# Re-planned stages in a wavelet convolution block with vector quantization: branch order, interleaved attention products, two upper-band steps on GpSimd, loop written out

## The reference

```python
x = x + conv_block(_gn(x), ...)      # _gn: per image and channel, mean and variance over all pixels
x = x + vq(_gn(x), codebook)

def conv_block(x, ...):
    LL, LH, HL, HH = _dwt_haar(x)                      # four 64x64 bands of 32 channels
    hf = concat([LH, HL, HH])
    x1 = lrelu(conv(lrelu(conv(hf, w15)), w25))        # 5x5
    x2 = lrelu(conv(lrelu(conv(hf, w13)), w23))        # 3x3
    x3 = lrelu(conv(lrelu(conv(hf, w12)), w22))        # 2x2
    y = lrelu(conv(x1 + x2 + x3, wd1, dil=2))          # then wd2, wd3, also dilated
    alpha = sigmoid(conv(y, wca))                      # 1x1, to 3 * 32 channels
    phf = alpha * hf
    z = batchnorm(conv(concat([LL, phf]), wcb))        # 3x3
    return _idwt_haar(z * sigmoid(z), conv(phf, whf), HL, HH)

def vq(x, codebook):                                   # 512 codes of 32 channels
    idx = argmin(|x|^2 - 2 x.codebook^T + |codebook|^2)
    return codebook[idx]
```

## Time and profile before

| | us |
|---|---|
| time, three runs | 2281.72, 2288.87 (median), 2294.78 |
| span of the profiled execution | 2164.4 |
| median less span | 124.5 |
| mean granted clock of TensorE | 0.951 |

### The profile page before, as it was taken

One profiled execution on the slowest core, in us unless ns is written; L12 is line 12 of the kernel. 1 busy time (PEld: TensorE's weight loads), 2 busy tenths in 40 slices (PEclk: granted clock), 3 DMA queues, 4 the chain that ended last, 5 costly groups with the idle time before them and its releaser, 6 DMA issues. The chain is left out here.

```text
span 2164.4 us, 27115 instructions
## 1 busy us (share of the span) xinstructions
PE 1984.8 (92%) x5232; PEld 946.5 (44%) x5232; DVE 1810.3 (84%) x3979; ACT 1059.2 (49%) x2018; POOL 1252.3 (58%) x1299
## 2 busy tenths in 40 slices
PE   6999999999999999999999999999999999995653
PEld 3444455444544455444544445444544445442221
DVE  4122799988999799988999899988999889888996
ACT  5134645545555545546556454546455454543331
POOL 2001277654776377663776367673776457673876
PEclk9999999999999999999999999999999999995555
DMA  6000011111110112111111111111111011110111
GB/s 203 15 10 5 20 40 43 27 29 34 46 35 21 41 36 47 25 24 41 42 36 26 42 35 41 30 24 37 43 41 26 20 25 34 30 25 20 34 37 32
DMA packets 80459, 76.97 MB, mean 36 GB/s; under 512 B 29200, under 2 KB 62608, under 8 KB 80016
## 3 DMA queue, kind: packets, MB, share of 16 engines
q1 hardware_dynamic: 45776, 50.78, 8.3%
q0 software_dynamic: 32768, 16.84, 5.2%
q10 hardware_dynamic: 1728, 7.41, 0.9%
HBM read 41.36 MB, written 16.78 MB: 27 GB/s over the span
## 5 line engine op out<-in xcount | busy, mean ns | idle before, releaser
L1053 POOL DMA_INDIRECT vqc<-in_codebook,idx x1024 | 1000.9, 977 | 545.2 <-DVE idx L964 306.4
L542 PE MATMUL ring<-hf,w_sb 128*128 128x512 f32 x1824 | 888.5, 600 | 2.9 <-ACT hf L715 2.9
L487 PE MATMUL score<-cst,yst 98*128 98x512 f32 x1024 | 788.4, 777 | 83.8 <-DVE idx L964 54.8
L960 DVE MAX8 top<-score 128x8 f32<-128x512 f32 x1024 | 695.3, 684 | 74.7 <-PE score L487 63.8
L964 DVE FIND_INDEX8 idx<-top,score 128x8 uint32<-128x512 f32 x1024 | 704.2, 690 | 0.0
L666 ACT CAST yst<-bands 32x256 fp32r<-32x256 f32 x1024 | 411.3, 402 | 174.6 <-PE score L487 162.1
L542 PEld LDWEIGHTS ring<-hf,w_sb 128*128 128x128 f32 x1824 | 341.6, 191 | 316.9 <-issue 294.2
L487 PEld LDWEIGHTS score<-cst,yst 98*128 98x128 f32 x1024 | 204.0, 202 | 395.0 <-DVE idx L964 206.3
L542 PE MATMUL ring<-ha,w_sb 128*128 128x512 f32 x704 | 347.5, 598 | 5.1 <-DVE ha L853 4.6
L542 PE MATMUL ring<-hb,w_sb 128*128 128x512 f32 x544 | 262.6, 595 | 6.8 <-DVE hb L866 6.8
L627 ACT ACTIVATE z<-ring,prm 128x512 f32<-128x512 f32 x144 | 99.0, 688 | 273.3 <-PE ring L542 272.7
(11 more groups left out here) (101 smaller groups left out, 1276.8 us busy)
## 6 DMA issues: line engine op xcount, KB each, us to landing
xnat<-in_x SPq DMA_DIRECT2D x128, 128.0 KB, 2.7
yst<-yl SPq DMA_DIRECT2D x512, 32.0 KB
vqc<-in_codebook,idx POOLq DMA_INDIRECT x1024
out<-vqc SPq DMA_DIRECT2D x128, 128.0 KB
w_sb<-in_weights ACTq DMA_DIRECT2D x1, 1920.0 KB, 8.2
w_sb<-in_weights ACTq DMA_DIRECT2D x3, 384.0 KB, 12.8
w_sb<-in_weights ACTq DMA_DIRECT2D x1, 1152.0 KB, 15.6
w_sb<-in_weights ACTq DMA_DIRECT2D x1, 960.0 KB, 8.6
```

Source lines behind the costliest of these rows:

```text
L487: nc.tensor.matmul(score[BANK["tile", t]][:, :], yst[0:KST, j % 2, g, wp], cst[0:KST, :], start=True, stop=True).then_inc(s_tile, 1)
L542: t = nc.tensor.matmul(ring[g % RING][:, :, :], w_sb[:, SLOTS[n, m, kind, ky], :], own(source(n, m, kind), half, slice(PAD + di, PAD + di ...
L960: nc.vector.max(top8[:, t % 4, :], score[BANK["tile", t]][:, :]).then_inc(s_top, 1)
L1053: nc.gpsimd.indirect_dma_start(vqc[:, c % 2, w * CH:(w + 1) * CH], None, codebook[:, :], bass.IndirectOffsetOnAxis(idx[:, c % 2, k, 0:1], ...
```

## The change

The parts, in the order of the plan:

- `ORDER` becomes w13, w12, w23, w22, w15, w25, wd1, wd2, wd3. `w22` is now added to `w23` (`branch_pair`), and `w25` to both (`branch_sum`). `LEAKY_TILE` puts w13 and w15 in `ha`, w12 in `hb`.
- `mean2`, `var2`, `bias2` stand before products 8, 12, 16. DVE's steps of `finish` and `finish_rest` are spread over `finish`, `mean2` and `var2`, the last of them between `veps` and the wait for `rstd`. ACT's `high` and POOL's `low` start with `var2`.
- `normal_side` (8 ACT instructions) moves to the end of the round before, `normal_edge` (6) from there to a new step `edge` before product 40.
- A new step `upper` before product 48: POOL computes the sum and the difference of HL and HH (before: DVE, at the end of the round). DVE's statistics of them move to a new step `spread` before product 58; only the LH step stays at the last `cbmap` (`upper_low`).
- `wcb`, `wca` and `whf` are interleaved; `wca` and `whf` share the two banks of `wd3`, `wcb` has those of `wd2` (`group_banks`, `freed_before`). `weighted_sides` is cut into three steps `wside`.
- Turns: `xchunk` before tiles with t % 16 = 9, `mean1` before tile 126, `var1` behind tile 127. Turns start before product 20; the EDGE products of half 1 without turns are those of w25, wd1, wd2, wd3.
- POOL issues each gather one tile later than before, with the same rule as `index`.
- `wait_apart` becomes `wait`: no semaphore step between the wait and its instruction.
- The loop of `rounds` is written out: nine bodies with constant numbers.

```diff
-XTURN = 10
-LEAD, REAR = 9, 16
+XTURN = 9
+LEAD, REAR = 8, 16
+EDGING = 40
...
-ORDER = ["w15", "w13", "w25", "w12", "w23", "w22", "wd1", "wd2", "wd3"]
+ORDER = ["w13", "w12", "w23", "w22", "w15", "w25", "wd1", "wd2", "wd3"]
...
+def group_banks():
+
+    banks = {key: g % RING for key, g in GROUP.items() if key[0] in ORDER}
+    for h in range(2):
+        last = banks["wd3", h]
+        for m in range(3):
+            banks["wca", m, h] = last
+        banks["whf", h] = last
+        banks["wcb", h] = banks["wd2", h]
...
-            if t == TILES - 4:
+            if t == TILES - 2:
                 turns.append(("mean1",))
-            if t == TILES - 2:
-                turns.append(("var1",))
             turns.append(("tile", t))
+    turns.append(("var1",))
...
+    def attention(m):
+        return [("mm", "wca", half, m, OWN, 0) for half in range(2)]
+
+    def map_of(m, halves=(0, 1)):
+        return [("mm", "wcb", half, m, OWN, ky) for half in halves for ky in range(3)]
+
+    def high_bands(m):
+        return [("mm", "whf", half, m, OWN, 0) for half in range(2)]
+
+    plan += map_of(0, (0,)) + attention(0) + map_of(0, (1,)) + [("cbmap", 0)] + attention(1)
+    plan += map_of(1) + attention(2) + [("wside", 0), ("wside", 1)]
+    plan += map_of(2) + high_bands(0) + [("cbmap", 1)] + high_bands(1) + [("cbmap", 2), ("wside", 2)]
+    plan += high_bands(2) + map_of(3) + [("cbmap", 3)]
...
-    at = {LEAD: [("mean2",)], LEAD + 6: [("var2",)], LEAD + 9: [("bias2",)], LEAD + 10: [("side",)]}
+    at = {LEAD: [("mean2",)], LEAD + 4: [("var2",)], LEAD + 8: [("bias2",)],
+          EDGING: [("edge",)], EDGING + 8: [("upper",)], EDGING + 18: [("spread",)]}
...
-def wait_apart(eng, sem, value, passed):
-
-
-    wait(eng, sem, value)
-    eng.sem_inc(passed, 1)
...
-            with eng.Fori(0, (IMAGES - 2) // 2) as i:
-                body(2 * i + 1, 1, True, True, True)
-                body(2 * i + 2, 0, True, True, True)
+            for b in range(1, IMAGES - 1):
+                body(b, b % 2, True, True, True)
...
+            def mean2(v, par):
+                statistics(1, v, s_dq, QSTEP * v + 1, 0, vpart[:, :])
+                quarter(raw(par, LH), resid, par).then_inc(s_dh, 1)
+                dve.wait_ge(s_dh, 2 * (v + 1))
+                quarter_rest(raw(par, HL), nresid, par)
+
+            def var2(v, par):
+                dve.wait_ge(s_var[1], v + 1)
+                nc.vector.tensor_scalar_add(veps[1][:, :], score[1][:, 0:1], GN_EPS).then_inc(s_veps[1], 1)
+                quarter_rest(raw(par, HH), resid, par).then_inc(s_band, 1)
+                dve.wait_ge(s_rstd[1], v + 1)
...
+            def upper(b, par):
+
+                pool.wait_ge(s_side, b + 1)
+                pool.wait_ge(s_hfw, 6 * (b + 1))
+                wait(pool, s_band, b)
+                nc.gpsimd.tensor_tensor(hsum[:, :, :], raw(par, HL), raw(par, HH), ALU.add).then_inc(s_up, 1)
+                pool.wait_ge(s_up, b + 1)
+                nc.gpsimd.tensor_tensor(raw(par, HH), raw(par, HL), raw(par, HH), ALU.subtract).then_inc(s_upper, 1)
...
+                        if pending is not None:
+                            gather(v, pending)
+                        pending = t
+                        if t in RUN_ENDS:
+                            gather(v, t)
+                            pending = None
```

More of the change, by code:

```diff
@@ L107, with freed_before @@
 RING = 4
-assert NG % RING == 0
+def group_banks():
[6 more added lines that the diff above has]
+        banks["wcb", h] = banks["wd2", h]
+    assert len({banks["wd3", 0], banks["wd3", 1], banks["wcb", 0], banks["wcb", 1]}) == RING
+    return banks
+GBANK = group_banks()
+def freed_before(b, key):
+    g = GROUP[key]
+    held = [NG * c + h for c in (b - 1, b) for k, h in GROUP.items()
+            if GBANK[k] == GBANK[key] and 0 <= NG * c + h < NG * b + g]
+    return max(held) + 1 if held else 0
 COL = {n: i for i, n in enumerate(["b15", "b13", "b12", "b25", "b23", "b22", "bd1", "bd2", "bd3", "bca0", "bca1",
@@ L181 @@
 LEAKY = ORDER
-HAS_EDGE = ["w15", "w13", "w12", "wd1", "wd2"]
+HAS_EDGE = ["w13", "w12", "w15", "wd1", "wd2"]
 def last_products():
@@ L498, in source @@
                     return hf[m][kind]
-                return {"w25": ha, "w23": hb, "w22": ha, "wd1": hb, "wd2": ha, "wd3": hb, "wca": ha}[n][kind]
+                return {"w25": ha, "w23": ha, "w22": hb, "wd1": hb, "wd2": ha, "wd3": hb, "wca": ha}[n][kind]
             def inputs_ready(b, n, half, m, kind):
-                if n == "w15" and half == 0:
-                    pe.wait_ge(s_hfw, 6 * b + (m + 1 if kind == 0 else m + 4))
+                if n == "w13" and kind == OWN and half == 0:
+                    pe.wait_ge(s_hfw, 6 * b + m + 1)
+                elif n == "w15" and kind == EDGE and half == 0:
+                    pe.wait_ge(s_hfw, 6 * b + m + 4)
                 elif n == "w13" and kind == LEFT and half == 0:
@@ L633, in evacuate @@
                         fill.then_inc(s_edge, 1)
-                    if half == 1 and n == "w22":
+                    if half == 1 and n == "w25":
                         act.wait_ge(s_sum, 2 * b + 2)
@@ L740, in body @@
                             xorder(b + 1, k)
[L741 removed]
+                    if quant and what == "var2":
                         for j in range(2):
@@ L759, in body @@
                         normal_ll(b + 1, 1 - par)
-                    elif conv and what == "side":
-                        normal_side(b, par)
-                    elif conv and what == "cbmap" and step[1] == 1:
-                        weighted_sides(b)
+                    elif conv and what == "edge":
+                        for m in range(3):
+                            normal_edge(b, par, m)
+                    elif conv and what == "wside":
+                        weighted_side(b, step[1])
                     elif conv and what == "mm":
```

145 lines of the change are left out of this document (63 added, 82 removed).

## The result

| | before | after |
|---|---|---|
| time, median of 6 runs, us | 2288.52 (2281.72 to 2294.78) | 2264.41 (2262.23 to 2268.85) |
| ratio | 1 | 0.9886, 95% interval 0.9864 to 0.9908 |
| span of the profiled execution, us | 2164.4 | 2263.3 |
| its own time less its span, us | not known | 1.8 |

The change makes the kernel 24 us (1.1%) faster, a small gain but clear of the noise, where 22 were forecast. But its span is 99 us *longer* than the one the prediction rests on. The two can't both be taken at face value, and most of what follows is about that.

What follows compares the result with a forecast made beforehand. PE bounds the kernel, DVE a close second. Six looped rounds -20 us, round 7 -1, round 0 -0.5, round 8 -0.5: -22 in all, span 2164.4 to 2142, plus 124.5 outside: 2267 us, range 2239 to 2302.

Steps and rivals of the forecast that it cites:

- The base: Whole kernel: span 2164.4 us, median 124.5 above it and held there; 12.5 us per looped round above PE's floor to win.
- Loop written out: Rounds 1 to 6: straight code costs nothing seen; gain only the 1.86 us idle at back edges, already counted.
- Semaphore steps: Separate steps behind waits: given no price; in round 8 the 0.30 us between gathers was taken as unchanged.
- Branch order: Convolution branches: wait before `wd1` goes, 1.2 us, and score-bank waits, 2.0 us, per looped round.
- Pile-up: Tiles 3 to 31: extra DVE work stops PE about 7.3 us per looped round (5.3 to 13.5).
- GpSimd's sum and difference: Products 49 to 56: POOL's 4.3 to 5.2 us hidden; DVE held 1 us, bounds 0 and 5.2.
- rival B: Products 49 to 56: POOL's sum and difference hold DVE; slower, 2298 to 2304 us; chance 0.15.
- Start of the round: First tiles: side copies moved and mean one product earlier gain some 3.1 us per looped round.
- Attention: Attention stage: covered waits gain 1.9 us per looped round, next image's later mean 1.9, half of `attend`'s hold on DVE 1.4.
- Round 8: Last round, set by POOL's gathers: gather spacing unchanged, round stays at 204 us; statistics gain 0.5.
- Rival C: Round 8: gathers get shorter, another 10 to 17 us lost, 2250 to 2257 us; chance 0.08.
- Rival A: Looped rounds: stop of 10.5 instead of 7.3 us, net about 0 to -1; 2280 to 2290; chance 0.27 with another rival.

Runs made afterwards that it cites:

- e0: The kernel before, unchanged, timed and profiled again: 2287.8 us, ratio 1.0012.
- e1: The kernel before with only the loop over rounds 1 to 6 written out: 2219.8 us, ratio 0.9733.
- e3: The kernel before with the loop written out and the separate semaphore steps taken out, old plan kept: 2200.5 us, ratio 0.9649.
- e7: The changed kernel with the old branch order, 5x5 branch first, and edge copies at place 18: 2212.3 us, ratio 0.9664.
- e12: The changed kernel with old branch order, edge copies at place 18, and upper bands' statistics, sum and difference on DVE at the round's end: 2188.1 us, ratio 0.9576.
- e4: The changed kernel with the upper bands' sum and difference made by DVE at the same place, not GpSimd: 2267.0 us, ratio 0.9932.
- e11: The changed kernel with old branch order, edge copies at place 18, upper bands' statistics at the round's end, and old attention order: 2235.2 us, ratio 0.9886.
- e6: The changed kernel with the attention stage's order and banks as before: 2279.8 us, ratio 0.9957.
- e8: The kernel before with loop written out and plain waits, plus the new attention order and banks: 2234.1 us, ratio 0.9762.

## Why the prediction was right in its number and wrong in its reasons

*The base.* The step that failed first is "Span 2164.4 to 2142. The median is 2288.9, 124.5 above the span; I hold that at 124.5, since no row shows it." The 124.5 us were not outside the span; they were stops inside it that this one execution lacked. So the "12.5 us per round above PE's floor" were 29 in e0 (its looped rounds, from 233.2 to 1816.8, are 263.9 us each, less 234.6), and the room to win was 176 us, not 75. A gap of 5% between a span and all times of the same kernel was in the table ahead of the prediction. The list of what would prove it wrong names "a time outside the span other than 124.5": it is 1.8.

*Loop written out: "its gain is the 1.86 us at back edges".* Measured 64 us, in e1. *Semaphore steps, no price:* 19 us, in e3. Together 83 us, more than three times what the whole change wins. What in the loop costs this (register reads in the waits, branches, fetching) wasn't isolated; the trace shows only that the late maxima fall from 103 to 60 us in all.

*Branch order: gain 3.2.* Two of its claims hold in the trace: at tiles 80 to 87 e3 shows waits of 1.0 us per round for `hb` ahead of `wd1` and 0.4 for score banks, after none. But the stop just ahead of them, at tiles 72 to 79, grew from 1.2 us of excess in e3 to 4.3, and e7 shows a loss of 8.0 us of excess per round, 51 us in all. The prediction did see that eight leaky steps and two pair sums come before tile 31, but booked the pile-up to the change as a whole and its gain to the order.

*Pile-up: 7.3 us (5.3 to 13.5), 50 to 75 us into the round.* Right in place (67 and 72 us into round 4), cause and about in size: 8.6 at tiles 24 to 39, 8.4 of excess in round 4 (the 9.3 of the expectations is too high), some 2 of it from the tail. By the prediction's own rows the statistics take 3.5 and not 3.3 us and the slack is 2.8 and not 3.0, together 0.4 us more. Not foreseen were that tail, 6.8 us at the low clock in each of rounds 1 to 7, and the stops at tiles 8 to 23 and 72 to 87. After has 72 us more at 0.50 than e3. Counted over the matmuls that start at 0.50 and have no wait behind them, the low clock costs after 31 us and e3 7: the difference, 24 us, is some four tenths of the plan's price.

*GpSimd's sum and difference: 1 us (0 to 5.2) for DVE, POOL's own time "hidden as such".* The first half held, against the rival B: in round 4 of after the two steps run from 1072.54 to 1077.34, DVE has only maxima and indices then, and these take 0.68 and 0.69 us as ever. The prediction's reading by the Trainium skill (SBUF — State Buffer, the section on its two separate sides) needs DVE steps with two SBUF inputs beside them. DVE's addition of 2.04 us above, held until POOL's own addition has ended, agrees with it, though its row starts 0.47 us before POOL's. The second half failed: POOL's 4.7 us delay its gathers by 5 us, and e12 shows what the two steps cost once the earlier stop is out of the way, 4.5 us of excess per round. In the changed kernel itself taking them off GpSimd gained nothing (e4).

*Start of the round: 3.1.* Start and tiles 0 to 7 went from 4.1 (e0) or 2.7 (e3) to 1.6: 2.5 or 1.1. Right in kind; in e0 a part of it was the loop's and the semaphore steps'.

*Attention, 1.9, mean 1.9, half of `attend`'s hold 1.4.* Tiles 104 to 127: 13.3 in e0, 9.8 in e3, 8.5 in after. So 1.3 of the 5.2 in straight code. The waits named are gone, but tile 109 now waits 2.53 us in round 4. As e11, e6 and e8 show, the part's worth runs from +31 over +15 to -34 us with what stands around it.

*Round 8: no change, 204.* 207.8 in after, 213.3 in e0, 212.3 in e1 and 208.4 in e3. So some 4 of the 5 us go with the semaphore steps and not with the loop; between two gathers there are 0.30 us as before. Rival C, 10 to 17 us of shorter gathers, is out.

*Rival A, "Pile-up eats the gain",* is what happened to the plan, with (B)'s sign: it ate more than the gain. That the forecast of 2267 met 2264 is luck, the sum of two errors of opposite sign: some 80 us that the code's form won and that were not in the sum, and 54 to 64 that the plan cost where it was booked as winning 22.

## What to carry to other kernels

Hold the span of the profiled execution against the times before taking any term from it; where they differ by more than a few us, that execution isn't the one to explain, and another profile is worth more than any reasoning. Take a change apart into code form and plan from the outset: here a written-out loop and plain waits carried three times the whole gain, and hid a plan that lost. When TensorE and DVE need almost the same time per tile, the order of the stages must spread DVE's extra steps. And an engine that has a gather of 1.25 us for each tile of 1.32 may be idle for four tenths of a round, but a step of 4.7 us put between the gathers is not made up for by the next 24 tiles.

## What the runs showed of the hardware

- *Signals arrive late at times.* In after a waiting maximum typically starts 0.84 us after its tile's start. In the first profile of before there are 5 places where DVE is idle and the maximum starts over 0.3 us later than that, in all other traces 22 to 67. Timelines of PE, then DVE, in round 4 of after:

```profile
1119.77 0.80 PE L506 MATMUL score<-cst,yst 98*128 98x512 f32 x1
...
1121.73 0.80 PE L506 MATMUL score<-cst,yst 98*128 98x512 f32 x1
...
1124.82 0.50 PE L506 MATMUL score<-cst,yst 98*128 98x512 f32 x1 [1.41 <-DVE idx L988]
```

```profile
1119.19 0.69 DVE L988 FIND_INDEX8 idx<-top,score 128x8 uint32<-128x512 f32 x1
1123.39 0.70 DVE L984 MAX8 top<-score 128x8 f32<-128x512 f32 x1 [3.51 <-PE score L506]
```

  TensorE's rows run on at their pace while DVE waits 3.51 us; the increments of the tiles at 1119.77 and 1121.73 are recorded at 1123.30 and 1123.37. Transfers are held up with them: no landing of a DMA is recorded from 1121.88 to 1123.30, and then 37 within 0.74 us. The places sum to 103 us in e0, 60 in e1, 54 in e3, 45 in after, 2.5 in the first profile; the 100 us between the two profiles of before are of the size of the 122 us between their spans. They don't explain the plan's price: after has less of them than e3. Nor are they random: they come at the same tiles round after round, 8 of after's 24 at tiles 48 and 49 and 11 at 64 to 70, in e0 6 at tile 10, 6 at 21 and 11 at 36 and 37. So something in the plan or in the transfers of those places is behind them; instruction fetches stand near only about 10 of e0's 67. Which it is stays open, and whether TensorE's rows or its signals are displaced can't be told from these traces either.
- *A stop of TensorE can cost more than itself.* Behind the pile-up the clock stood at 0.50 for 6.8 us, with a product's matmuls 0.85 us apart in place of 0.435. Without the first profile (7 us and 2164), the traces with less than 35 us at clock 0.50 in rounds 1 to 7 have spans of 2182 to 2214, those with over 80 us 2263 to 2295; but the stops themselves come with both, so this doesn't give the low clock's own price.
- *One chip of four ran the kernel before in 2257.7 us*, 26 to 29 us faster than the other three.
- *GpSimd's small step is held too.* In after, `rstd` (128x1) takes 0.55 us at the least and up to 1.54 where DVE's step L932 (two inputs of 128x1024) runs beside it; that step takes 1.27 in all eight rounds.
